# Output products one step later, routing's products one step earlier, and a remainder moved up VectorE's queue, in a gated cross-attention and mixture-of-experts kernel

## The reference

```
x = x + tanh(g_xattn) * attn(layernorm(x), ctx)        # 16 heads, rotary keys, clip, softmax, @ Wo + bo
  attn = softmax(clip(q k^T / 8, -11, 11)); out = attn @ v; return out @ Wo + bo
x = x + tanh(g_ffn) * moe(layernorm(x))
  scores = sigmoid(x @ router_w.T); choose 4 of 8 groups, then 8 of 64 experts; weights normed, * 2.5
  moe = sum over chosen experts of w * (relu(x @ up)^2 @ down) + shared expert
```

## Time and profile before

| | us |
|---|---|
| median of 3 runs | 2553.73 |
| lowest and highest | 2549.09 and 2558.55 |
| profiled execution | 2553.1 |
| its span | 2551.4 |
| mean granted TensorE clock in it | 0.968 of full |

### The profile page before, as it was taken

The page is one execution under the profiler, slowest core; times in us unless marked ns, Lnnn a source line. Parts: engine busy times, 40 slices in busy tenths (PEclk is TensorE's granted clock), DMA queues, the critical chain, the costliest instruction groups (busy, mean ns, idle before and its releaser), DMA issues. The chain is left out here.

```text
span 2551.4 us, 40379 instructions
## 1 busy us (share of the span) xinstructions
PE 2294.6 (90%) x11366; PEld 1273.0 (50%) x11366; DVE 2055.1 (81%) x3571; ACT 1524.2 (60%) x2556; POOL 1734.6 (68%) x1515
## 2 busy tenths in 40 slices
PE   3999999999999999998999999999986989999980
PEld 2444445444444444344444444444443668987770
DVE  4778688978988897889789888978886759688884
ACT  4667666656666666666566666665662334766660
POOL 2767676588859876976788498759874700177776
PEclk9999999999999999999999999999997999999995
DMA  9533433111111112111112111111114428799994
GB/s 345 200 104 130 163 118 120 38 60 57 61 48 58 46 55 68 58 58 49 56 46 72 39 68 44 58 47 62 55 44 149 162 93 289 256 324 320 326 321 132
DMA packets 163585, 306.30 MB, mean 120 GB/s; under 512 B 19779, under 2 KB 99587, under 8 KB 160643
## 3 DMA queue, kind: packets, MB, share of 16 engines
q1 hardware_dynamic: 135234, 235.93, 27.1%
q0 software_dynamic: 24576, 67.14, 8.0%
q10 hardware_dynamic: 3520, 0.27, 0.1%
HBM read 173.51 MB, written 129.76 MB: 119 GB/s over the span
## 5 line engine op out<-in xcount | busy, mean ns | idle before, releaser
L1139 POOL TENSOR_SCALAR e<-e 128x1024 f32<-128x1024 f32 x512 | 689.8, 1347 | 357.5 <-ACT e L1047 303.6
L1047 ACT ACTIVATE e<-scores 128x1024 f32<-128x1024 f32 x512 | 525.1, 1026 | 410.9 <-PE scores L903 398.2
L1286 DVE TENSOR_TENSOR e_sum<-e_sum,e 128x1024 f32<-128x1024 f32 x384 | 585.7, 1525 | 160.7 <-POOL e L1139 151.9
L968 PE MATMUL ps_o<-e,v 128*64 128x512 f32 x2048 | 560.8, 626 | 7.0 <-POOL e L1139 6.6
L903 PE MATMUL scores<-q_t,k_t 64*128 64x512 f32 x3072 | 499.9, 431 | 4.7 <-issue 4.7
L903 PEld LDWEIGHTS scores<-q_t,k_t 64*128 64x128 f32 x3072 | 251.4, 186 | 365.2 <-issue 293.2
L1839 POOL DMA_INDIRECT more<-results_in_blocks,index x256 | 248.2, 970 | 256.9 <-DMA results_in_blocks<-more 175.2
L1065 ACT ACTIVATE k_sw<-ps_k 32x512 f32<-32x512 f32 x512 | 301.7, 589 | 89.8 <-PE ps_k L944 84.8
L1119 POOL DMA_INDIRECT rows_in_blocks<-room,a_r_index_now x192 | 267.7, 1394 | 49.0 <-issue 46.2
L944 PE MATMUL ps_k<-ctx_t,wqk 128*128 128x512 f32 x768 | 219.4, 422 | 34.1 <-DVE q_t L1264 34.1
L1131 POOL TENSOR_TENSOR k_c<-k_c,k_sw 128x512 f32<-128x512 f32 x128 | 199.6, 1559 | 32.6 <-DVE k_sw L1271 29.1
(11 more groups left out here) (288 smaller groups left out, 3511.4 us busy)
## 6 DMA issues: line engine op xcount, KB each, us to landing
rows_in_blocks<-room SPq DMA_DIRECT2D x16, 2560.0 KB, 10.4
x_nat<-rows_in_blocks SPq DMA_DIRECT2D x160, 256.0 KB
results_in_blocks<-more SPq DMA_DIRECT2D x80, 512.0 KB, 3.9
wqk<-wqk_pairs SPq DMA_DIRECT2D x65, 512.0 KB, 3.6
wv<-wv_quads SPq DMA_DIRECT2D x17, 1024.0 KB, 4.8
x_nat<-in_ctx SPq DMA_DIRECT2D x9, 1024.0 KB, 7.7
wo<-in_L_xattn_Wo SPq DMA_DIRECT2D x66, 128.0 KB, 3.6
down_all<-in_L_ffn_down_w SPq DMA_DIRECT2D x16, 512.0 KB, 7.1
```

The source lines that it names most:

```text
L968: mm = pe.matmul(ps_o[hh * DH:(hh + 1) * DH, :], v[:, tile, buf, hh * DH:(hh + 1) * DH], e[:, tile % 4, hh * N:(hh + 1) * N], start=(tile ...
L1047: act.activation(e[:, c % 4], scores[:, c % 2], ACT.Exp, scale=SCALE).then_inc(s_exp, 1)
L1139: pool.tensor_scalar(e[:, c % 4], e[:, c % 4], EXP_HI, EXP_LO, ALU.min, ALU.max).then_inc(s_clip, 1)
L1286: dve.tensor_tensor(total, e[:, 0] if c == 2 else total, e[:, tile % 4], ALU.add).then_inc(s_sum, 1)
```

## The change

- TensorE: the two output products of a pair move from the ends of steps 4 and 6 to the ends of steps 5 and 7 (`OUT`).
- TensorE: routing's products move from step 5 to step 4 of pairs 2, 3, 4 and 6. They stood behind the first output product and waited for its addition (`s_add`); now they stand ahead of it and wait for the Newton step (`s_rec`). ScalarE's copies of them move from step 6 to step 5.
- VectorE: the additions to `x1` move with the products. The first half is added at the start of step 6 (before: 5), the second at the start of the next pair's step 0 (before: step 7).
- VectorE: the first `normalise` of routing moves from step 4 to step 3 of pair 2.
- VectorE: the queries' remainder moves from the start of step 3 to step 2, directly behind the Newton step and ahead of what routing does in step 2.

```diff
@@ -763,7 +763,7 @@
         s_oraw, s_on, s_out, s_add = sem("s_oraw"), sem("s_on"), sem("s_out"), sem("s_add")
 
         SUM_READ = [1, 2, 3, 4, 5, 5, 6, 7]
-        OUT = {4: 0, 6: 1}
+        OUT = {5: 0, 7: 1}
         FINISH = (1, 2, 4, 6, 7)
         CHUNKS = 6
         CHUNK_AT = {(7, 3): 0, (7, 4): 1, (7, 5): 2, (7, 6): 3, (7, 7): 4, (0, 0): 5}
@@ -977,19 +977,19 @@
                                        start=True, stop=True)
                     mm.then_inc(s_den, 1)
 
-                if routed(b) and c == 5 and p in (2, 3, 4, 6):
-                    pe.wait_ge(s_add, 2 + g * 2 + 1)
+                if routed(b) and c == 4 and p in (2, 3, 4, 6):
+                    pe.wait_ge(s_rec, g + 1)
                     if p in (2, 3):
                         router.turn(pe, b - 1, p - 2, y_flat)
                     elif p == 4:
                         router.logits(pe, b - 1, y_flat)
                     else:
                         router.rank(pe, b - 1, y_flat)
-                if routed(b) and c == 6 and p in (2, 3):
+                if routed(b) and c == 5 and p in (2, 3):
                     pe.wait_ge(router.copied, (b - 1) * 2 + p - 1)
-                if routed(b) and c == 6 and p == 4:
+                if routed(b) and c == 5 and p == 4:
                     pe.wait_ge(router.tanh_done, b)
-                if routed(b) and c == 6 and p == 6:
+                if routed(b) and c == 5 and p == 6:
                     pe.wait_ge(router.ranks_kept, b)
 
                 if c in OUT and tail:
@@ -1202,6 +1202,14 @@
 
             numbered = [None]
 
+            def add_result(g, half):
+                dve.wait_ge(s_out, 2 + g * 2 + half + 1)
+                batch = ((g + 6) // PAIRS + B - 1) % B
+                rows = (pers.x1[:, batch * NT + 2 * half:batch * NT + 2 * half + 2, :] if isinstance(g, int) else
+                        pers.x1[:, bass.ds(batch * NT + 2 * half, 2), :]).rearrange("p a n -> p (a n)")
+                dve.scalar_tensor_tensor(out=rows, in0=y_flat, scalar=minus_gate[:], in1=rows,
+                                         op0=ALU.mult, op1=ALU.add).then_inc(s_add, 1)
+
             def route(b, p, c, g):
                 r = b - 1
                 if not isinstance(b, int) and p == 0 and c in FINISH:
@@ -1219,7 +1227,7 @@
                     router.add_bias(dve, r, 1)
                     router.statistics(dve, range(2, 4))
                     router.aggregate(dve)
-                if (p, c) == (2, 4):
+                if (p, c) == (2, 3):
                     router.normalise(dve, 0)
                 if (p, c) == (2, 6):
                     router.normalise(dve, 1)
@@ -1251,17 +1259,10 @@
             def step(g, m, c, project, attend, b=None, p=None):
                 jj = m % 2
                 tail = exists(g - 2)
-                if c - 1 in OUT and tail:
-                    half = OUT[c - 1]
-                    dve.wait_ge(s_out, 2 + g * 2 + half + 1)
-                    batch = ((g + 6) // PAIRS + B - 1) % B
-                    rows = (pers.x1[:, batch * NT + 2 * half:batch * NT + 2 * half + 2, :] if isinstance(g, int) else
-                            pers.x1[:, bass.ds(batch * NT + 2 * half, 2), :]).rearrange("p a n -> p (a n)")
-                    dve.scalar_tensor_tensor(out=rows, in0=y_flat, scalar=minus_gate[:], in1=rows,
-                                             op0=ALU.mult, op1=ALU.add).then_inc(s_add, 1)
-                if project and c == 3:
-                    dve.wait_ge(s_qe, g + 1)
-                    dve.tensor_tensor(q_t[:, jj, 1], ps_k[:], f32(q_t[:, jj, 0]), ALU.subtract).then_inc(s_qlo, 1)
+                if c == 6 and tail:
+                    add_result(g, 0)
+                if c == 0 and exists(g - 3):
+                    add_result(g - 1, 1)
                 if project and c in (1, 5):
                     half = c // 4
                     tokens = slice(half * N, (half + 1) * N)
@@ -1290,6 +1291,9 @@
                     dve.wait_ge(s_part, g + 1)
                     dve.scalar_tensor_tensor(out=r_den[:], in0=o_n[:], scalar=2.0, in1=r_den[:],
                                              op0=ALU.subtract, op1=ALU.mult).then_inc(s_rec, 1)
+                if project and c == 2:
+                    dve.wait_ge(s_qe, g + 1)
+                    dve.tensor_tensor(q_t[:, jj, 1], ps_k[:], f32(q_t[:, jj, 0]), ALU.subtract).then_inc(s_qlo, 1)
                 chunk = chunk_at(b, p, c) if project else None
                 if chunk is not None:
                     split_rows(*chunk)
@@ -1299,6 +1303,7 @@
                     finish_slots(B - 2, FINISH.index(c))
 
             loop(dve, step, prepare=prepare)
+            add_result(B * PAIRS + 1, 1)
 
 
 def four_blocks(dram, i):
```

## The result

The changed kernel takes 2511.76 us (median of 4 runs, 2507.92 to 2517.10) against 2556.12 us (median of 4, 2549.09 to 2558.55) for the kernel before on the same chip. The ratio is 0.9836, with a 95% interval of 0.9819 to 0.9854: 42 us faster by the ratio, 44 by the medians.

A forecast was written before the change was run, and what follows sets the result against it. VectorE or GpSimd, not TensorE, was taken as the bound in stretches of the attention; gains of 11.7 + 1.6 + 3.4 + 4.9 + 3.5 = 25.1 us off 2553.1, plus 0.6, gave 2528.6 us, range 2500 to 2554.

The forecast's parts named there:

- The remainder in pair 0 and the clock behind it: TensorE's six waits for the remainder end, 11.7 us, and the slow clock in the key projection behind them, 1.6 us.
- The remainder in pair 5: TensorE's wait for the queries' remainder in pair 5 ends and is gained whole: 3.4 us.
- The remainder in pair 7: TensorE resumes about 2 us earlier, but only idle time in VectorE's queue is gained: 0.7 us seven times, 4.9 us.
- But VectorE's queue is no shorter: Pair 7: VectorE's work stays as long, so TensorE's 2 us return as waits at the fourth split and e_sum.
- Pair 2: TensorE's waits become one of about 2.3 us at the transpose; earlier normalise helps VectorE: 0.5 us seven times, 3.5 us.
- Routing's products: Pairs 3 and 6: their waits for the addition end, but full VectorE and GpSimd queues leave 0 gained, bound 14.9 us.
- VectorE is full until 1196: Pair 7, behind rank: VectorE waits nowhere for TensorE, so earlier routing products gain 0.
- In its place the waits of ps_y for e_sum should be about 2 us longer: Pair 0, step 1: the denominators' product should wait about 2 us longer per batch once the remainder's wait is gone.
- Rival A: TensorE is the bound throughout, so all 34.1 and 14.9 us of waits come back: 2504.7 us; chance 0.18.
- B: VectorE and GpSimd swallow the gains, in pair 0 too; little but pair 5's 3.4 us stays: 2550 us; chance 0.18.
- C: Pair 2: normalise beside GpSimd's o_n takes 2.25 us, delaying the transpose 1.1 us seven times: 2536 us; chance 0.13.
- D: Slower: the second output product, at step 7's end, waits for the first half's addition; 1 us late gives 2593 us; chance 0.09.

The follow-up runs named there:

- e3: The kernel before with the queries' remainder moved directly behind the Newton step in pair 0 only: 2535.24 us, ratio 0.9938.
- e4: The kernel before with the queries' remainder moved directly behind the Newton step in pair 7 only: 2539.76 us, ratio 0.9946.
- e5: The kernel before with GpSimd's clips of two tiles in pair 7 cut to 8 of 1024 columns, their exponential's scale quartered: 2536.40 us, ratio 0.9934.
- e6: The changed kernel with the same cut of two clips and of the exponential's scale in pair 7: 2507.35 us, ratio 0.9820.
- e2: The changed kernel with the queries' remainder put back at the start of step 3, all other moves kept: 2521.93 us, ratio 0.9876.
- e7: The changed kernel with the addition of the result's first half moved, in pair 7 only, to the end of VectorE's step 5: 2502.94 us, ratio 0.9799.
- e12: The kernel of e7 unchanged, run again on another chip where the kernel before took 2691.96 us: 2634.50 us, ratio 0.9800.

## Why the prediction was right, and where not

**The sign** was right, and the time in the stated range; it was 17 us too high, a gain of 25.1 us forecast and 42 to 44 us measured. The forecast's mechanism (waits of TensorE that end, and only some of which return) held; the sum was mis-sized. That the total is no further off is in part luck: apart, the remainder gave 27.5 us for 21.6 and the rest of the change 31.6 us for 3.5, and an overlap of 17 us, nearly all of it in pairs 0 and 7 and not foreseen either, took back part of the excess. Term by term:

- *The remainder in pair 0 and the clock behind it*, 13.3 us: 19.4 us came in pair 0 with both parts in, 15.6 us with this one alone (e3). The wait is gone, and nothing came in its place. Read one by one, the six waits are 12.3 us (and those of pair 7 are 18.0, of pair 5 3.8); the 11.7 were a difference from one batch's rows. Besides, VectorE comes into pair 0 earlier than before, which e4 shows apart (5.2 us in pair 0 from an edit in pair 7).
- *The remainder in pair 5*, 3.4 us: 4.4 us. Right.
- *The remainder in pair 7*, 4.9 us: 13.8 us alone (e4). The step that failed is "What is really gained is the idle time left in VectorE's queue", counted as 0.7 us a batch. It was 0.56 + 0.96 us in the batch that was read, the second part one row past where the prediction stopped reading, and 1.5 to 3.6 us over the seven batches, 2.5 in the mean.
- *"But VectorE's queue is no shorter"*: this failed for the whole change. The stretch of pairs 6 and 7 was 4.5 us shorter, 2.4 us a batch of it (2.8 in the batch read) because four short instructions meet less of GpSimd's (e5, e6). The prediction priced such meetings for the normalise alone, as a loss.
- *Pair 2*, 3.5 us: 2.5 us. Near, with the wait 0.8 us longer than forecast, a longer stretch at the low clock, and all 1.28 us at pair 3's start gone where 0.5 were counted.
- *Routing's products*, 0 with 14.9 us as the bound: in pair 6, 5.9 us came (products alone, e2, the same 5.9). "VectorE is full until 1196" was true and no reason. At the end of pair 6 TensorE did not wait for VectorE, and after the change it does. The product of the denominators there, before and after:

```profile
1165.87 1.08 PE L976 MATMUL ps_y<-e_sum,ones_dh 128*64 128x512 f32 x4
```

```profile
1145.36 1.08 PE L976 MATMUL ps_y<-e_sum,ones_dh 128*64 128x512 f32 x4 [0.68 <-DVE e_sum L1287]
```

So of the 1.47 us that the ranks waited for the addition, 0.68 came back and 0.8 did not. That pair 7 did not give up the 0.8 goes with VectorE's shorter stretch above; no run shows that link apart.
- *"In its place the waits of ps_y for e_sum should be about 2 us longer"*: they are not; in pair 0 the product of the denominators no longer waits at all. By the prediction's own words this speaks for A, and pair 0 did go A's way. But the sign misleads: in the changed kernel the wait and the gap at the branch (0.62 + 2.92 us) and the slow clock stand just ahead of that product, where it would have waited; and in e4, where they do not, 2.14 us stand at the split in place of the forecast 2 us at e_sum.

Rival A (2504.7 us) was nearest in time and wrong in its reason: pairs 2 and 7 still wait for VectorE and GpSimd. B fell with e3. C happened at 0.8 us a batch; what it cost was not taken apart, and pair 2 still gained. D happened in one pair of eight, at 0.62 us, and drew a gap of 2.9 us and a slow clock behind it: some 9 to 14 us (e7, e12), a third to a half of the 25.1 us that its condition would have cost over 64 pairs. Nothing in the prediction spoke of what the branch costs TensorE, and it should have: the product was moved from step 6 to the last place ahead of it.

## What to carry to other kernels

- Busy time is not work. Where an instruction's mean is several times that of its twin in another place, look at what the neighbour engine does beside it, before taking a full queue for a fixed length; a move elsewhere can shorten it or stretch it.
- A wait that stands last ahead of a loop's branch costs more than itself here: the gap behind it grew from 0.5 to 0.9 us to some 3 us, by my reading because the fetch behind the branch is then uncovered. Put work that is sure to be ready there, and take the wait a step ahead (e7: one addition moved, 9 us).
- When counting the slack of an engine behind a wait, follow it until the engine that follows has caught up, not to the first wait that returns, and do so in every batch: the one read here had 1.5 us, the mean was 2.5.
